# Transposes by DMA in two 16 bit halves in place of TensorE products with the identity, in a fused cross-attention and ternary feed-forward kernel

## The reference

```python
h0 = layernorm(x)                                    # no gain, no bias
h1 = ln(h0 + mha(h0, h0, h0, s_w*, mask_s), ln1)     # self attention, 16 heads of 16
h2 = ln(h1 + mha(h1, ctx, ctx, c_w*, mask_x), ln2)   # cross attention
f  = relu(h2 @ ff_w1 + ff_b1) @ ff_w2 + ff_b2        # 256 -> 1024 -> 256
x1 = x + tanh(g_xattn) * ln(h2 + f, ln3)
h4 = layernorm(x1)
# bitlinear(a, w): a rounded per row to 8 bit steps, w to -1, 0, 1 times its mean
gate, up = bitlinear(h4, w_gate), bitlinear(h4, w_up)          # 256 -> 1024
out = x1 + tanh(g_ffn) * bitlinear(silu(gate) * up, w_down)    # 1024 -> 256
```

## Time and profile before

| | |
|---|---|
| profiled execution's own time | 1026.44 us |
| its span, first to last instruction | 1024.5 us |
| median of three timed runs | 1021.93 us |
| busy: TensorE, VectorE, ScalarE, GpSimd | 867.8, 788.5, 637.9, 591.2 us |
| mean granted TensorE clock | 0.934 of full speed |
| DMA: bytes moved, mean share of the 16 engines (queue q1) | 77.71 MB, 36.7% |

### The profile page before, as it was taken

One profiled execution on the slowest core, in us unless ns is written; L12 is line 12 of the kernel. 1 busy time (PEld: TensorE's weight loads), 2 busy tenths in 40 slices (PEclk: granted clock), 3 DMA queues, 4 the chain that ended last, 5 costly groups with the idle time before them and its releaser, 6 DMA issues.

```text
span 1024.5 us, 26372 instructions
## 1 busy us (share of the span) xinstructions
PE 867.8 (85%) x10089; PEld 708.1 (69%) x10147; DVE 788.5 (77%) x1903; ACT 637.9 (62%) x996; POOL 591.2 (58%) x630
## 2 busy tenths in 40 slices
PE   0327678989999999999999999999999999978565
PEld 0215457777878787878787878787878787766443
DVE  7654566668888888888888888888888888867454
ACT  1125254647677777777777767777777777764433
POOL 7004245566666666676767675757585858471520
PEclk9956696999999999999999999999999999989785
DMA  6251434343434343443444434343535352121000
GB/s 178 83 113 43 83 74 75 84 74 74 90 80 90 79 91 79 82 88 75 94 74 96 74 90 79 85 86 79 90 75 85 85 84 73 25 68 18 21 11 10
DMA packets 131755, 77.71 MB, mean 76 GB/s; under 512 B 10121, under 2 KB 131120, under 8 KB 131633
## 3 DMA queue, kind: packets, MB, share of 16 engines
q1 hardware_dynamic: 131632, 76.04, 36.7%
HBM read 54.49 MB, written 20.98 MB: 74 GB/s over the span
## 4 chain that ended last, share of the span: by engine, by line
PE 44%; DVE 16%; POOL 13%; DMA 10%; SPq 7%; issue 6%; ACT 3%; POOLq 0%; DVEq 0%; ACTq 0%
DMA stk_AQ<-parts_AQ 9%; PE lin_C L671 7%; SPq L583 6%; PE lin_A L671 4%; PE lin_E L671 4%; PE lin_B L671 4%; POOL elo L1343 3%; PE smax L750 3%; PE st L774 3%; DVE lst L1112 3%; POOL lrs L1323 2%; POOL late L1374 2%; PE smax L746 2%; POOL late L1366 2%; DVE nm_A L1162 2%
## 5 line engine op out<-in xcount | busy, mean ns | idle before, releaser
L1343 POOL TENSOR_TENSOR elo<-e,ehi 128x1024 f16<-128x1024 f32 x128 | 273.8, 2139 | 149.7 <-ACT ehi L943 149.4
L1323 POOL TENSOR_TENSOR lrs<-lve,neghalf 128x1 f32<-128x1 f32 (+1 forms) x112 | 70.9, 633 | 199.8 <-DVE lve L1121 195.5
L941 ACT ACTIVATE e<-st 128x1024 f32<-128x1024 f32 x128 | 130.1, 1017 | 45.1 <-PE st L774 44.0
L943 ACT ACTIVATE ehi<-st 128x1024 f16<-128x1024 f32 x128 | 129.8, 1014 | 0.0
L1162 DVE TENSOR_REDUCE nm_B<-smax 128x4 f32<-128x512 f32 x128 | 87.6, 684 | 20.0 <-PE smax L750 19.9
L1162 DVE TENSOR_REDUCE nm_A<-smax 128x4 f32<-128x512 f32 x128 | 87.7, 685 | 19.2 <-PE smax L750 18.5
L671 PE MATMUL lin_C<-w,late 128*128 128x256 f16 x768 | 90.0, 274 | 0.0
L671 PEld LDWEIGHTS lin_C<-w,late 128*128 128x128 f16 x768 | 75.7, 99 | 8.8
L746 PE MATMUL smax<-mb,ident_big 128*128 128x512 f16 x128 | 52.2, 408 | 18.5 <-DMA stk_AQ<-parts_AQ 9.8
L750 PE MATMUL smax<-stk_BK,stk_BQ 126*128 126x128 f16 x512 | 50.7, 222 | 9.0 <-DVE nm_B L1162 5.9
L750 PEld LDWEIGHTS smax<-stk_AK,stk_AQ 126*128 126x128 f16 x512 | 42.2, 102 | 18.3 <-issue 4.1
(11 more groups left out here) (284 smaller groups left out, 2827.3 us busy)
## 6 DMA issues: line engine op xcount, KB each, us to landing
stk_AK<-parts_AK SPq DMA_DIRECT2D x64, 128.0 KB, 4.0
stk_AQ<-parts_AQ SPq DMA_DIRECT2D x64, 128.0 KB, 5.6
stk_BK<-parts_BK SPq DMA_DIRECT2D x64, 128.0 KB, 3.7
stk_BQ<-parts_BQ SPq DMA_DIRECT2D x64, 128.0 KB, 3.7
x_a<-in_x_dram SPq DMA_DIRECT2D x16, 256.0 KB, 2.8
cx<-in_ctx_dram SPq DMA_DIRECT2D x16, 256.0 KB, 2.7
parts_AK<-qk_AK SPq DMA_DIRECT2D x16, 256.0 KB, 2.2
parts_AQ<-qk_AQ SPq DMA_DIRECT2D x16, 256.0 KB, 2.5
```

The costliest lines, as they stand in the source:

```text
L941: eng.activation(e32[:, hf, :], st[:, :], ACT.Exp, scale=SCORE).then_inc(e32_ready, 1)
L943: eng.activation(ehi[:, hf, :], st[:, :], ACT.Exp, scale=SCORE).then_inc(st_drained, 1)
L1323: eng.tensor_tensor(lrs[n][:, a:b], lve[n][:, a:b], neghalf[:, 0:b - a], ALU.pow).then_inc(ln_rstd[n], 1)
L1343: eng.tensor_tensor(elo[:, hf, :], e32[:, hf, :], ehi[:, hf, :], ALU.subtract).then_inc(elo_ready, 1)
```

## The change

Each transpose in the steps T, X, O, TQ and DN is made by a transposing DMA that SP issues, from SBUF to SBUF, on two-byte elements:

- T and X: ScalarE copies h (or the context) from SBUF to the fp16 high part hl[:, 0], GpSimd subtracts to the low part hl[:, 1], and one `dma_start_transpose` turns both (8 blocks of 128x128) into hT. Four of these per group.
- O: the same with ol and oT, 4 blocks, once per sequence. ScalarE and GpSimd form the halves, where ScalarE and VectorE did.
- TQ: ScalarE casts the quantised activation to bf16 (q1h), one transfer of 4 blocks makes q1T.
- DN: the steps DN 0 and DN 1 go. A new step TD casts the 1024 columns of q2m to bf16 (q2h), one transfer of 8 blocks makes q2T, and DN is only the product.

SP's list therefore carries 11 more transfers per group. Each waits for its source parts, and for the readers of the transposed tile in the use before.

```diff
+                elif name in ("T", "X"):                      # SP
+                    s, n = what[0], use(g, step)
+                    eng.wait_ge(hl_lo[s], n + 1)
...
+                    for reader in readers:
+                        wait(eng, *st_.full(reader, back=0 if step == ("Bp", "T") else 1))
+                    eng.dma_start_transpose(hT[s][:, :, :, :, :].rearrange("p q b c n -> p (q b c) n"),
+                                            hl[s][:, :, :, :].rearrange("p q b d -> p (q b d)")).then_inc(hT_in[s], 16)
...
+                elif name == "O":
+                    b = step[2]
+                    eng.wait_ge(ol_lo[what], G * g + b + 1)
+                    wait(eng, *(st_.full((what, "W", 0)) if b else st_.full((what, "W", G - 1), back=1)))
+                    eng.dma_start_transpose(oT[what][:, :, :, :].rearrange("p q c n -> p (q c) n"),
+                                            ol[what][:, :, :].rearrange("p q d -> p (q d)")).then_inc(oT_in[what], 16)
+                elif name == "TQ":
+                    eng.wait_ge(q1h_ready, g + 1)
+                    wait(eng, *st_.full(("E", "GU", G - 1, 3), back=1))
+                    eng.dma_start_transpose(q1T[:, :, :, :].rearrange("p b c n -> p (b c) n"), q1h[:, :]).then_inc(q1T_in, 16)
+                elif name == "TD":
+                    k = step[2]
+                    eng.wait_ge(q2h_ready, G * g + k + 1)
+                    wait(eng, *(st_.full(("E", "DN", 0)) if k else st_.full(("E", "DN", G - 1), back=1)))
+                    eng.dma_start_transpose(q2T[:, :, :], q2h[:, :]).then_inc(q2T_in, 16)
```

```diff
-                    for c in range(DC):                       # TensorE, T and X
-                        for b in range(G):
-                            at = c * T + b * P
-                            mm = eng.transpose(bank[:, at:at + P], src[:, b, c * P:(c + 1) * P], ident[:, :])
...
-                if name in ("T", "X"):                        # VectorE
-                    i_ = eng.tensor_tensor(whole(hT[s][1]), bank[:, :], whole(hT[s][0]), ALU.subtract)
...
+                    eng.activation(hl[s][:, 0, :, :], (cx if name == "X" else hin[s][g % 2])[:, :, :],
+                                   ACT.Copy).then_inc(hl_hi[s], 1)                          # ScalarE
...
+                elif name in ("T", "X"):                      # GpSimd
+                    s = what[0]
+                    eng.wait_ge(hl_hi[s], use(st_.g, st_.step) + 1)
+                    eng.tensor_tensor(hl[s][:, 1, :, :], (cx if name == "X" else hin[s][st_.g % 2])[:, :, :],
+                                      hl[s][:, 0, :, :], ALU.subtract).then_inc(hl_lo[s], 1)
```

```diff
-            last = BCOL["ff_b2"]
-            setup(eng.tensor_scalar(bf[:, 0:last], bf[:, 0:last], WS, None, ALU.mult), u_b1, n_b1)
-            setup(eng.tensor_scalar(bf[:, last:NBIAS], bf[:, last:NBIAS], WS * WS, None, ALU.mult), u_b1, n_b1)
-            setup(eng.tensor_copy(bhi, bf), u_b1, n_b1)
-            setup(eng.tensor_tensor(blo, bf, bhi, ALU.subtract), u_b1, n_b1)
+                elif what == "rows":
+                    eng.wait_ge(u_bias, 16 * len(BIASES))
+                    setup(eng.tensor_scalar(bhi, bq, WS, None, ALU.mult), u_split, 1)
+                    eng.scalar_tensor_tensor(blo, bq, WS, bhi, ALU.mult, ALU.subtract).then_inc(u_split, 1)
...
-    return START[g] + AT[step] + LATE.get((engine, step), 0.0)
+    return START[g] + AT[step] + LATE.get((engine, step), 0.0) + TWEAK.get(item, 0.0)
```

More of the change, by code:

```diff
@@ L89 @@
     + [("E", n) for n in ("norm", "amax", "quant", "TQ")] + [("E", "GU", k, j) for k in range(G) for j in range(4)]
-    + [("E", "Q2", k) for k in range(G)] + [("E", "DN", k, j) for k in range(G) for j in range(3)]
+    + [("E", what, k) for k in range(G) for what in ("Q2", "TD", "DN")]
+)
+PREPARE = (
+    [("set", n) for n in ("const", "rows", "mask", "flags", "gate", "scales")]
+    + [("set", "w", n) for n in range(10)] + [("set", "load", n) for n in range(9, 13)] + [("set", "bv", i) for i in range(2)]
+    + [("set", "stk", s, t) for s in "AB" for t in "QK"]
+    + [("set", n, m) for n in ("abs", "mean", "scale", "clip") for m in range(3)]
+    + [("set", "turn", m, r) for m in range(3) for r in range(2)]
@@ L250, in half @@
     return halves // 2
-def jobs_before(bank, m, part):
-    here = ORDER["PE"].index((m, ("setup", part)))
-    return sum(1 for item in ORDER["PE"][:here] if lane_of(item[1]) == bank)
 def check_order():
@@ L599, in _ @@
                 what, name = step[0:2]
-                if what == "setup":
-                    if name == 1 and g < 2:
-                        late_load(11 + g)
+                if what == "set":
+                    prepare(*step[1:3])
                 elif name in ("inK", "inQ"):
@@ L618, in _ @@
                         eng.dma_start(x_a[:, :, :], x_v[g + 1]).then_inc(x_in, 16)
[L619 to L622 removed]
+                elif step[0:2] == ("E", "DN"):
                     eng.wait_ge(*st_.read(step))
@@ L646, in ternary @@
[L646 to L663 removed]
+            eng.wait_ge(u_const, N_FIRST)
@@ new lines, in prepare @@
+            def prepare(st_, what, n=0, r=0):
+                bank, fill, drain, before, after = st_.job()
+                wait(eng, drain, before)
+                if what == "flags":
+                    eng.wait_ge(u_dve, 10)
+                    eng.transpose(bank[:, :].bitcast(F16)[:, 0:P], mb[:, :], ident16[:, :])
+                    eng.matmul(bank[:, P:2 * P], ones[:, :], scr[:, :], start=True, stop=True, skip_group_check=True)
+                    mm = eng.matmul(bank[:, 2 * P:2 * P + NB], ones[0:NB, :], scr2[0:NB, 0:NB], start=True, stop=True,
+                                    skip_group_check=True)
+                elif what == "bv":
+                    eng.wait_ge(u_bvb, n + 1)
+                    eng.wait_ge(u_raw[4 * n + 3], LOADED)
+                    for c in range(DC):
+                        mm = eng.matmul(bank[:, 0:D], bvb[:, c, :], raw[4 * n + 3][:, c * D:(c + 1) * D],
+                                        start=(c == 0), stop=(c == DC - 1))
+                elif what == "mean":
+                    eng.wait_ge(u_abs, n + 1)
+                    mm = eng.matmul(bank[:, 0:1], ones[:, :], rs3[:, n:n + 1], start=True, stop=True)
+                else:
+                    eng.wait_ge(u_const, N_CONST)
+                    eng.wait_ge(u_clip, 2 * n + 2)
+                    half_bank = bank[:, :].bitcast(BF16)
+                    for k in range(8):
+                        blk = r * 8 + k
+                        mm = eng.transpose(half_bank[:, k * P:(k + 1) * P], wq16[:, blk * P:(blk + 1) * P], identb[:, :])
+                mm.then_inc(fill, 1)
@@ L793, in values @@
                 mm.then_inc(av_filled, 1)
-            def output_rows(st_, s, b):
-                bank, fill, drain, before, after = st_.job()
-                wait(eng, drain, before)
-                eng.wait_ge(av_drained, half(count("values", st_.g, (s, "values", b, 1))))
-                for c in range(DC):
-                    mm = eng.transpose(bank[:, c * P:(c + 1) * P],
-                                       o[s][:, c * HB:(c + 1) * HB, :].rearrange("p h d -> p (h d)"), ident[:, :])
-                mm.then_inc(fill, 1)
             def project(st_, s, b):
@@ L839, in beside @@
                 mm.then_inc(fill, 1)
-            eng.wait_ge(u_lo, 8)
-            eng.wait_ge(u_dve, 13)
-            eng.wait_ge(u_w, 48)
-            for s in "AB":
-                eng.wait_ge(u_stk[s], 4)
             for st_ in program("PE"):
                 what, name = st_.step[0:2]
-                if what == "setup":
-                    ternary(st_.g, name)
+                if what == "set":
+                    if lane_of(st_.step):
+                        prepare(st_, *st_.step[1:])
                 elif name == "smax":
@@ L964, in quantised @@
                     eng.wait_ge(q_small, 5 * g + 5)
-                    wait(eng, *st_.full(("E", "TQ"), back=1))
+                    wait(eng, q1h_ready, g)
                     for b in range(G):
@@ L984, in quantised @@
                     eng.activation(tanhg[:, :], bank[:, :], ACT.Tanh, scale=hcg[:, k:k + 1]).then_inc(tanh_ready, 1)
-                elif name == "DN" and j < 2:
-                    bank, fill, drain, before, after = st_.job()
-                    eng.wait_ge(fill, after)
-                    eng.activation(q2T[:, 4 * j:4 * j + 4, :].rearrange("p f n -> p (f n)"), bank[:, :], ACT.Copy,
-                                   bias=-MAGIC).then_inc(drain, 1)
             for st_ in program("ACT"):
                 g, (what, name) = st_.g, st_.step[0:2]
-                if what == "setup":
-                    ternary(g, name)
+                if what == "set":
+                    prepare(*st_.step[1:3])
                 elif what in "AB" and name in ("scores", "M", "O", "N"):
```

729 lines of the change are left out of this document (391 added, 338 removed), and 245 rows, old and new, of tables (AT, BANK, LATE, TWEAK).

## The result

The changed kernel took 1113.24 us (median of 4, 1107.57 to 1128.86), the kernel before 1020.82 us (1019.15 to 1024.56): ratio 1.089, 95% interval 1.082 to 1.096, 92 us slower. Forecast were 948 us and a range of 900 to 1060 us. Single executions of some kernels fall into a slower state; these (the highest of the four here and in x7, the two highest of four in x6) are left out of the ratios and, in x6, of what the text works out.

What follows compares the result with a forecast made beforehand. TensorE was taken as the bound, 50.4 us busy of a 52.15 us period. From 1026.4 us, - 70 (periods) - 15 (setup) - 10 (ramp) + 21 (latency) gave 952.4, less 4.5 to the median: 948 us; range 900 to 1060.

Steps and rivals of the forecast that it cites:

- TensorE is the bound, so its saving comes off the period (- 70 us): Steady state: removing 44 TensorE transposes per group shortens each of 15 periods by 4.65 us, to 47.5 us, saving 70 us.
- no one wait rules: Chain that ended last: its largest piece, the gather of stacked queries, holds 9%, so no single wait was taken to dominate.
- TensorE falls to 44.7 us: TensorE per group: removing the transposes saves 5.7 us, so its busy time falls from 50.4 to 44.7 us.
- rival B: SP queue: transposes at its head delay gathers, the clock could slip, the period stays at 51.5 us; 1018 us, chance 0.20.
- VectorE 40.5, ScalarE no change, GpSimd 42.6 us: Work per group: VectorE falls from 44.9 to 40.5 us, ScalarE nets zero, GpSimd rises from 35.3 to 42.6 us.
- The charge for GpSimd, 1.2 us of one period: GpSimd's order: a new piece standing ahead of an elo that value products wait for costs 1.2 us per period.
- The DMA engines, 39 us, 30 ns a packet: DMA engines per group: 68 blocks add 16 us at 30 ns a packet to 23 us, fitting in 47.5 us.
- rival C: Transposes fill the DMA engines: 75 ns per packet, 64 us per group, 1226 us in total; chance 0.15.
- The SP queue, nothing beyond latency: SP: eleven added transposes cost 4 to 22 us of issuing per group, but nothing is charged beyond latency.
- The latency of a group, + 21 us: Passage of group 15: seven transpose steps in a row, each 3 us longer by DMA, add 21 us; bounds 17 and 41.
- Setup - 15, ramp - 10: Start: shorter setup work brings first statistics near 24 us, saving 15 us; the new order of early and late groups saves 10.

Runs made afterwards that it cites:

- x7: The changed kernel with the row-maximum DMA (four per group) issued by ScalarE in place of SP; 1144.83 us, ratio 1.117.
- x6: The changed kernel without its eleven DMA transposes per group, products waiting for the feeding copies instead; 1067 us for the two lowest executions, median 1076.07 us.
- x11: The kernel before with each step's TensorE transposes replaced by one 16-bit identity product, order and copies kept; 1031.11 us, ratio 1.0065.
- x12: The changed kernel in its new order without DMA transposes, the ScalarE and GpSimd steps that fed them cut to 16 columns; 1048.20 us.
- x4b: The kernel before, its TensorE transposes kept, plus eleven transposing DMAs per group from SP that nobody reads; 1111.28 us, ratio 1.086.
- x1: The changed kernel with each transposing DMA replaced by an ordinary DMA of the same bytes, same queue, places and waits; 1105.66 us, ratio 1.081.
- x13: The changed kernel's instructions in the order of the kernel before, without DMA transposes, the steps that fed them cut to 16 columns; 1074.36 us.
- x2: The changed kernel with each transposing DMA replaced by a tiny ordinary DMA of 16 rows of 128 elements; 1081.93 us.
- x10: The changed kernel with five row-maximum products of stage A moved by 0.01 to 0.04 of a period in groups 3 to 12; 1122.10 us.

## Why the prediction was wrong

**TensorE is the bound, so its saving comes off the period (- 70 us).** This is the step that failed. "TensorE is idle only 1.6 us in a period" was right as a reading and wrong as a bound. x11 takes 2.5 us of work away (of the 5.7 in the term) with the order, the queues and all copies unchanged, and the period goes from 52.15 to 52.6 us. Something else holds the period at once; that it is the loop through gathers, maxima and the fixed orders, about as long as TensorE's work and hidden by TensorE at 97%, is my reading and not isolated by a run. In place of 4.65 us less the period became 4.1 us longer. By the table's spacings it grows from 52.15 to 53.2 us in the new order with the feeding steps cut (x12), to 54.4 with them (x6), and to 56.2 with the DMAs. The earlier trace rows had a hint, the gather at the head of the chain, and I passed over it with "no one wait rules".

**TensorE falls to 44.7 us.** The rows L703, L709, L801 and L834 are gone, but the work is 48.2 us in 56, with the clock granted at 0.85 to 0.91. Less the some 6 us that this clock adds by the estimate above, the work is near the forecast or below it. I had the clock only as a worry in rival B.

**VectorE 40.5, ScalarE no change, GpSimd 42.6 us.** Measured 42.0, 35.8 and 39.8 us in 56 us, so near. The charge for GpSimd, 1.2 us of one period, was put on the wrong thing: the price is that a product now waits for ScalarE, then GpSimd, both in order. Cut to 16 columns, these steps give back 22 us between the profiled executions (x6 to x12), 19 of them in the 15 periods.

**The DMA engines, 39 us, 30 ns a packet.** The 68 blocks took 13.1 us in place of 16, and the total by the share is 0.61 x 56.2 = 34 us. Right, and rival C is ruled out here: 24 ns, where it needed 45. By the Trainium skill, "Advanced Engine Details and Errata", X-Bar Transpose (TRN2), a transposing transfer is as fast as an ordinary one. For the landing that nearly holds, 2.7 against 2.3 us for hT_B, but not for the issue, 1.25 against 0.49 us, nor for the time of the DMA engines, 13.1 against 6.2 us per group. The 1309 ns that the Trainium skill gives for a block in "VectorE: DVE Perf Modes", The three transpose paths, does not add up block by block: eight of them landed in 2.7 us.

**The SP queue, nothing beyond latency.** Wrong in kind. An issue takes 1.2 us, inside my 0.4 to 2.0. In the old order such issues with their load cost 90 us (x4b) with no reader. In the new order, made with room for them, the form of the DMA costs 8 us by the medians (x1; 23 between the profiled executions) and all the DMAs together about 45 (x6). "SP waits more than half the time" is no reason for nothing: what counts is who stands behind at that moment.

**The latency of a group, + 21 us.** The passage grew by 42. The DMAs are 17 of it (245 to 228, x6), near my own figure, the feeding steps 3.5 (228.0 to 224.5, x12), and 21 stay when both are gone. x13 and x12 do the same work, 209 in the old and 225 in the new order: most of that rest is the order, which spreads a group over more of the others. I had counted added latencies in an unchanged order. But an order that hides a landing in the periods does so by starting things earlier and ending them later.

**Setup - 15, ramp - 10.** First statistics at 28.5 us, 10.4 us earlier and inside the bounds. In x2 and x6 they start at 24 us, my mark. The ramp gave nothing: group 0 took 244 us from its first statistics to its last output step, where it took 242.

**The range and the chances.** The result lies 53 us above the range. Rival B had the right direction and the right sentence, that transposes at the head of the queue push the gathers and the clock could slip, but took the old period as its worst. No case let a change that relieves TensorE and VectorE make the period longer unless the DMA engines filled up. This is the case that was missing.

**What stays open.** x12 has no more work on any engine in a period than the kernel before, but a lower clock (0.90 against 1.00 in the middle), and a period 1 us longer. Which cycle of waits sets 53.2 us there, or 52.15 before, no run isolates. Nor is it known whether another order for the new code would beat the old kernel; x10 and x7, two attempts by hand, did not make it faster. How much of the lengthened TensorE time is cause and how much effect is open too.

## What to carry to other kernels

An engine busy 97% of a period isn't shown to be its bound: take some of its work away at unchanged order and see if the period moves; here that one run, made first, would have put 70 us of forecast gain in doubt. In a kernel whose order is fixed by hand or by a planner, moving a step to an in-order queue costs what stands behind it, and a new order that hides the added latencies returns them in the passage of the last group. Look at the largest wait with suspicion: taken away, it may come back under two other names.

## What the runs showed of the hardware

- A transposing DMA held SP for 1.21 us with 4 blocks of 128x128 (oT_A, median) and 1.25 us with 8 (hT_B), an ordinary one of the same bytes for 0.49 us. The time hardly grew with the size.
- The transposing form raises the packets: 276,646 on the queue against 157,094 for ordinary DMAs of the same 111.7 MB, and the engines' share from 45.0% to 53.9%. For the 68 blocks of a group that is 13.1 us of the 16 engines in place of 6.2 (x1 and the kernel after, each against x2).
- TensorE gave back about a third of a saving by its clock: 2.5 us of work less per period, 0.8 us lost to a granted clock of 0.97 in two of four windows (x11).
